# Latent attention: the value products of two steps in one group at every odd step

## The reference

```python
c_q, c_kv = rmsnorm(x @ Wq_down), rmsnorm(x @ Wkv_down)      # 48 and 64 wide
q, k, v   = c_q @ Wq_up, c_kv @ Wk_up, c_kv @ Wv_up          # 16 heads of 128
q_rope, k_rope = rope(x @ Wq_rope), rope(x @ Wk_rope)        # 16 heads of 64
attn = softmax((q @ k.T + q_rope @ k_rope.T) * scale)
out  = (attn @ v) @ Wout
```

## Time and profile before

| | us |
|---|---|
| median of three runs | 2213.99 (2212.3 to 2214.46) |
| the profiled execution | 2221.23 |
| its span | 2219.5 |
| PE busy | 1996.0 (90%) |
| DVE busy | 1276.7 (58%) |
| ACT busy | 817.4 (37%) |
| POOL busy | 867.5 (39%) |
| latent attention, about | 1141 to 2150 of the span |

### The profile page before, as it was taken

One profiled execution on the slowest core, in us unless ns is written; L12 is line 12 of the kernel. 1 busy time (PEld: TensorE's weight loads), 2 busy tenths in 40 slices (PEclk: granted clock), 3 DMA queues, 4 the chain that ended last, 5 costly groups with the idle time before them and its releaser, 6 DMA issues. The chain is left out here.

```text
span 2219.5 us, 29901 instructions
## 1 busy us (share of the span) xinstructions
PE 1996.0 (90%) x8700; PEld 1249.6 (56%) x8701; DVE 1276.7 (58%) x2970; ACT 817.4 (37%) x1549; POOL 867.5 (39%) x684
## 2 busy tenths in 40 slices
PE   5899958898888789986779999999999999999987
PEld 5566635455554756654545555555566555555556
DVE  6322275777775722216656666666656666667525
ACT  2122244554555212223324444444523444444423
POOL 0344311231112034441115556555424555665631
PEclk9999968999899689996769999999999999999999
DMA  9111232232220811124141122222032222212101
GB/s 385 48 58 63 55 126 29 29 44 43 29 29 1 341 52 63 57 54 179 21 95 45 47 57 57 57 57 57 12 75 54 56 58 57 50 44 50 31 1 51
DMA packets 60570, 150.63 MB, mean 68 GB/s; under 512 B 12976, under 2 KB 18304, under 8 KB 58176
## 3 DMA queue, kind: packets, MB, share of 16 engines
q1 hardware_dynamic: 50208, 120.43, 20.6%
q0 software_dynamic: 9120, 24.92, 3.6%
q10 hardware_dynamic: 1152, 4.19, 0.5%
HBM read 68.95 MB, written 18.61 MB: 39 GB/s over the span
## 5 line engine op out<-in xcount | busy, mean ns | idle before, releaser
L1834 POOL TENSOR_TENSOR mla_PS<-mla_PS,mla_PT 128x1024 f32<-128x1024 f32 x192 | 458.4, 2388 | 200.2 <-ACT mla_PT L2120 198.8
L2263 DVE TENSOR_REDUCE mla_MXP<-PS 128x1 f32<-128x512 f32 x512 | 334.4, 687 | 199.7 <-PE PS L1915 197.5
L2120 ACT ACTIVATE mla_PT<-PS 128x512 f32<-128x512 f32 x512 | 293.5, 599 | 421.0 <-PE PS L1935 375.4
L1944 PE MATMUL PS<-mla_PT,mla_CN 128*64 128x512 f32 x1024 | 274.2, 614 | 0.0
L521 DVE COPY moe_HT<-PS 128x512 f32<-128x512 f32 x92 | 63.7, 692 | 307.0 <-PE PS L644 301.2
L1915 PE MATMUL PS<-mla_KH,mla_QH 113*128 113x512 f32 x512 | 199.2, 456 | 18.0 <-DMA mla_KL<-mla_SL 17.8
L675 POOL DMA_INDIRECT moe_XS<-rows_in,moe_GI x96 | 93.7, 976 | 307.5 <-PE PS L630 171.3
L1935 PE MATMUL PS<-mla_QH,mla_KH 113*128 113x512 f32 x512 | 210.3, 411 | 1.7 <-ACT mla_QH L2104 1.5
L1935 PE MATMUL PS<-mla_QL,mla_KH 113*128 113x512 f32 x512 | 201.8, 394 | 0.0
L1935 PE MATMUL PS<-mla_QH,mla_KL 113*128 113x512 f32 x512 | 201.7, 394 | 0.0
L1140 ACT ACTIVATE att_PT<-PS 128x1024 f32<-128x1024 f32 (+1 forms) x192 | 152.3, 812 | 95.2 <-PE PS L975 93.4
(11 more groups left out here) (297 smaller groups left out, 3192.4 us busy)
## 6 DMA issues: line engine op xcount, KB each, us to landing
W<-in_W_dram SPq DMA_DIRECT2D x16, 2048.0 KB, 28.0
mla_QH<-mla_SH SPq DMA_DIRECT2D x64, 128.0 KB, 2.4
mla_KH<-mla_SH SPq DMA_DIRECT2D x64, 128.0 KB, 2.4
mla_QL<-mla_SL SPq DMA_DIRECT2D x64, 128.0 KB, 2.5
mla_KL<-mla_SL SPq DMA_DIRECT2D x64, 128.0 KB, 2.4
mla_KH<-mla_SH SPq DMA_DIRECT2D x64, 96.0 KB, 2.4
mla_KL<-mla_SL SPq DMA_DIRECT2D x64, 96.0 KB, 2.4
sums_Y<-rows_out SPq DMA_DIRECT2D x9, 512.0 KB, 6.0
```

The lines of the kernel that those rows point to most:

```text
L1834: pool.tensor_tensor(PS[:, :], PT[:, slot(0), :] if k == 1 else PS[:, :], PT[:, slot(k), :], ALU.add).then_inc(s_ps.handle, 1)
L1944: ins = pe.matmul(bank(6)[h * DKVL:(h + 1) * DKVL, :], CN[:, b, k, 0:DKVL], PT[:, slot(k), h * HB:(h + 1) * HB], start=(k == 0), stop=(k = ...
L2120: act.activation(PT[:, slot(k), h * HB:(h + 1) * HB], bank(st_bank(s, h))[:, :], ACT.Exp, scale=MLA_SCALE).then_inc(s_p.handle, 1)
L2263: dve.tensor_reduce(MXP[:, n // NPC, c, h, t:t + 1], bank(piece_bank(n))[:, :], AX_X, ALU.max).then_inc(s_mx.handle, 1)
```

## The change

It has these parts, all in the functions `pair` and what they call; each instruction of a pair is still there, on the same engine and with the same operands.

- On PE, `values_of` for steps s-1 and s stands at the end of every odd step s, one after the other; even steps have none. The value unit of step 15, which stood in step 0 of the next pair, is now in step 15.
- The denominators of the block before move from step 0 to step 1 (ahead of the two value units). Those of step 8 stay there and now stand without a value unit behind them.
- `scores_of` takes the head as an argument. From step 10 on, two late pieces stand between the scores of head 0 and head 1 and two behind those of head 1; before, two stood ahead of the value unit and two behind it. At steps 1 to 9 all pieces stand ahead of the value units.
- `EARLY` is {3: 1, 4: 2, 5: 3} instead of {2: 1, 3: 1, 4: 2, 5: 2}; the banks of the early pieces change turns, and piece 26 waits for fewer maxima.
- `project(it + 1, 0, 1)` moves from step 0 to step 1, `project(it + 1, 1, 1)` stands ahead of its step's pieces, `max_rows` moves from step 6 to 7 and from 14 to 15.
- On DVE, the four reciprocals of step 0 spread over steps 1 and 2, between rotation and low parts; `latent_out` is behind them; the products of step 5 move to 4, `rotated` of step 6 to 5, the low parts of step 7 to 6 and 7.
- On ACT the high parts move: two before the exponential of step 2, one after that of step 3, two after that of step 6, one after step 7; `out_copy` stands ahead of the exponentials of steps 0 and 8.

```diff
-    LATE, EARLY = {9: 2, 10: 4, 11: 4, 12: 4, 13: 4, 14: 4, 15: 4}, {2: 1, 3: 1, 4: 2, 5: 2}
+    LATE, EARLY = {9: 2, 10: 4, 11: 4, 12: 4, 13: 4, 14: 4, 15: 4}, {3: 1, 4: 2, 5: 3}
-    piece_bank = lambda n: (A, E)[n % 2] if n >= NLATE else (C, E, B)[n % 3]
+    piece_bank = lambda n: (E, A)[n % 2] if n >= NLATE else (C, E, B)[n % 3]
...
@@ PE, pair
                             near = (it, buf) if s < TB else (it + 1, 1 - buf)
-                            scores_of(it, buf, s, first)
+                            for h in range(2):
+                                scores_of(it, buf, s, h, first)
+                                if s > TB + 1:
+                                    rough_scores(*near, todo[2 * h:2 * h + 2])
...
-                            if s == 0 and not last:
-                                pe.wait_ge(s_mx.handle, s_mx.at(2 * NPC * it + NLATE - 2))
-                                project(it + 1, 0, 0)
+                            if s < 2 and not last:
+                                pe.wait_ge(s_mx.handle, s_mx.at(2 * NPC * it + NLATE - 2 + s))
+                                project(it + 1, 0, s)
                             if s == 8:
                                 denominators(2 * it)
-                            rough_scores(*near, todo[:before])
-                            if s == 0 and not first:
-                                denominators(2 * it - 1)
                             if not last:
                                 if s == 3:
                                     project(it + 1, 0, 2)
+                                if s == 4:
+                                    project(it + 1, 1, 1)
+                            if s <= TB + 1:
+                                rough_scores(*near, todo[:1])
+                            if not last:
                                 if s == 5:
                                     project(it + 1, 1, 0)
                                 if s == 7:
                                     project(it + 1, 1, 2)
-                                if s == 14:
+                            if s <= TB + 1:
+                                rough_scores(*near, todo[1:])
+                            if s % 2:
+                                if s == 1 and not first:
+                                    denominators(2 * it - 1)
+                                if s == 7:
+                                    max_rows(it, 1)
+                                if s == NS - 1 and not last:
                                     pe.wait_ge(s_la.handle, s_la.at(2 * it + 1))
                                     max_rows(it + 1, 0)
-                            if s or not first:
-                                values_of(NS * it + s - 1, 2 * it + (s - 1) // TB, (s - 1) % TB)
...
+                                for done in (s - 1, s):
+                                    values_of(NS * it + done, 2 * it + done // TB, done % TB)
@@ DVE, pair
-                            if s == 5 and not last:
+                            if s == 4 and not last:
                                 products(it + 1, 1, 1)
                             if s == 6:
                                 block_max(it, 1)
-                            if s == 6 and not last:
-                                rotated(it + 1, 1)
+                                if not last:
+                                    lows(it + 1, 1, (0, 1))
+                            if s == 7 and not last:
+                                lows(it + 1, 1, (2,))
                             maxima(near, todo[:1])
                             if s == 5 and not last:
                                 products(it + 1, 1, 0)
+                                rotated(it + 1, 1)
```

More of the change, by code:

```diff
@@ L1923, in max_rows, with scores_of @@
                         ins.then_inc(s_mt.handle, 1)
-                    def scores_of(it, buf, s, first):
+                    def scores_of(it, buf, s, h, first):
                         q, k = s // TB, s % TB
-                        if k == 0:
+                        u = 2 * s + h
+                        if k == 0 and h == 0:
                             pe.wait_ge(s_nm.handle, s_nm.at(2 * (2 * it + q + 1)))
+                        if not (first and u < 3):
+                            pe.wait_ge(s_p.handle, s_p.at(NU * it + freed_unit(u)))
                         qs, ks = slice(q * HB, (q + 1) * HB), slice(k * P, (k + 1) * P)
-                        for h in range(2):
-                            u = 2 * s + h
-                            if not (first and u < 3):
-                                pe.wait_ge(s_p.handle, s_p.at(NU * it + freed_unit(u)))
-                            for n, (kk, qq) in enumerate(((KH, QH), (KH, QL), (KL, QH))):
-                                ins = pe.matmul(bank(st_bank(s, h))[:, :], kk[USED, buf, h, ks], qq[USED, buf, h, qs], start=(n == 0), stop=(n == 2))
-                            ins.then_inc(s_st.handle, 1)
+                        for n, (kk, qq) in enumerate(((KH, QH), (KH, QL), (KL, QH))):
+                            ins = pe.matmul(bank(st_bank(s, h))[:, :], kk[USED, buf, h, ks], qq[USED, buf, h, qs], start=(n == 0), stop=(n == 2))
+                        ins.then_inc(s_st.handle, 1)
                     def values_of(step, blk, k):
@@ L1972, in pair @@
                             todo = pieces_of(s, last)
-                            before = 0 if s == TB + 1 else len(todo) // 2
                             near = (it, buf) if s < TB else (it + 1, 1 - buf)
@@ L2128, in pair @@
                         for s in range(NS):
+                            if s == 0 and not first:
+                                out_copy(2 * it - 1)
+                            if s == 8:
+                                out_copy(2 * it)
                             if not last:
                                 if s == 2:
-                                    highs(it + 1, 0, (1,))
-                                if s == 7:
-                                    highs(it + 1, 1, (1,))
-                                if s == 8:
-                                    highs(it + 1, 1, (2,))
+                                    highs(it + 1, 0, (0, 1))
                                 if s == 12:
@@ L2138, in pair @@
                             exp_of(it, s, first and s < 3)
-                            if s == 0 and not first:
-                                out_copy(2 * it - 1)
                             if not last:
-                                if s == 1:
-                                    highs(it + 1, 0, (0,))
-                                if s == 2:
+                                if s == 3:
                                     highs(it + 1, 0, (2,))
                                 if s == 6:
-                                    highs(it + 1, 1, (0,))
-                                if s == 14:
+                                    highs(it + 1, 1, (0, 1))
+                                if s == 7:
+                                    highs(it + 1, 1, (2,))
+                                if s == NS - 1:
                                     max_copies(it + 1, 1 - buf, 0)
@@ L2296, in pair @@
                                     normalized(after, j)
-                            if s == 0:
-                                if not last:
-                                    products(it + 1, 0, 0)
-                                if not first:
-                                    reciprocals(2 * it - 1, (2, 3, 0, 1))
+                            if s == 0 and not last:
+                                products(it + 1, 0, 0)
+                            if s == 1:
                                 if not last:
                                     products(it + 1, 0, 1)
-                            if s == 1 and not first:
-                                latent_out(2 * it - 1, r - 1, 1)
-                            if s == 5 and not last:
+                                    rotated(it + 1, 0)
+                                if not first:
+                                    reciprocals(2 * it - 1, (2,))
+                                if not last:
+                                    lows(it + 1, 0, (0, 1))
+                                if not first:
+                                    reciprocals(2 * it - 1, (3, 0))
+                            if s == 2:
+                                if not last:
+                                    lows(it + 1, 0, (2,))
+                                if not first:
+                                    reciprocals(2 * it - 1, (1,))
+                                    latent_out(2 * it - 1, r - 1, 1)
+                            if s == 4 and not last:
                                 products(it + 1, 1, 1)
```

34 lines of the change are left out of this document (6 added, 28 removed).

## The result

| | before | after |
|---|---|---|
| median (8 runs each) | 2213.05 us | 2234.85 us |
| lowest to highest | 2212.19 to 2215.53 | 2222.32 to 2240.41 |
| the profiled execution | 2221.23 | 2237.49 |
| its span | 2219.5 | 2235.8 |

The ratio is 1.0090, with a 95% interval of 1.0073 to 1.0106: 20 to 22 us slower. The forecast was +6.3 us, 2220.5, with a range of 2204 to 2236. Direction and place were right; the size is more than three times what I gave. The range held by a narrow margin, and with some luck: the median is 1.2 us under its upper end, three of the eight executions are over it, and the narrower range of my own case, 2215 to 2229, misses the median. The runs of the changed kernel also lie 18 us apart, those of the kernel before 3.3.

A forecast was written before the change was run, and what follows sets the result against it. PE sets the pace, with a once-a-pair loop through the placing DMAs about as long. Twelve middle pairs +5.5, first pairs +3.4, last pairs -1.1 and -1.5 gave +6.3 us: 2220.5, range 2204 to 2236.

The forecast's parts named there:

- my own case: Whole kernel: PE's saving is outweighed by waits, chiefly for placing DMAs; +6.3 us, range 2215 to 2229, chance 0.48.
- The gain: PE's value units and denominators: 16 groups become 9, saving 0.34 each, 2.4 us a pair, if nothing else moved.
- Step 1: Middle pair, first scores of step 0 to step 6: 24.31 becomes 23.74 us.
- the wait of piece 29: At step 4 PE waits 0.3 us (bounds 0 and 0.6) for the maximum of piece 27, delayed by DVE's products.
- Steps 2 and 3: Step 6 to high parts, 3.26, then to piece 0, 9.59 us; PE, there after 11.0, waits 1.8 for placing DMAs.
- Step 4: Piece 0 to step 10: 0.57 becomes 2.42 us, since two value units now stand behind the pieces.
- Step 5: Step 10 to the next step 0: 21.48 becomes 20.56 us; late pieces wait for no maxima.
- First pairs: Two first pairs, with no unit left over from before: five single units become three double ones, +1.7 us each.
- Last pairs: Pairs without placing for their own batch: -1.1 us in batch 1, -1.5 in batch 0, each bounded by 0 and -2.5.
- High parts, reciprocals and out_copy: High parts at steps 2 and 3, reciprocals and out_copy, moved on ACT and DVE, were to cost nothing.
- rival C: PE's clock falls behind the wait at piece 0: 2246 if all 14 pairs lose 1.8 us, 2224 to 2230 if few; chance 0.12.

The follow-up runs named there:

- e10: e5 with the value units taken apart again, one a step, except at steps 7 and 15, which keep two: 2243.16 us, ratio 1.0130 to the kernel before.
- e5: e1 with DVE's products of step 4 put behind the maxima of pieces 27 and 28: 2186.88 us, ratio 0.9885 to the kernel before.
- e1: Changed kernel, but at step 9 the value units of steps 8 and 9 stand ahead of pieces 0 and 1: 2193.56 us, ratio 0.9931.
- e9: Changed kernel, but ACT makes two high parts of half 1 ahead of the exponentials of step 6: 2187.39 us, ratio 0.9878.
- e4: Kernel before, but at step 9 pieces 0 and 1 stand ahead of the value unit of step 8, nothing joined: 2231.64 us, ratio 1.0099.
- e6: e1 with the four late pieces of steps 10 to 15 all behind both heads' scores: 2244.18 us, ratio 1.0145 to the kernel before.
- e7: e1 with the four reciprocals of step 1 in one piece ahead of the rotation: 2246.52 us, ratio 1.0155 to the kernel before.
- e2: Changed kernel with six further score products at step 9 in the 14 pairs that prepare a next one: 2224.49 us, ratio 1.0062.
- e8: Changed kernel with six further score products a pair at step 12, where PE doesn't wait: 2250.48 us, ratio 1.0186.
- e11: e1, e5 and e9 together, with the latent keys of step 3 behind the piece: 2174.99 us, ratio 0.9822 to the kernel before.
- e3: Changed kernel, but ACT instead of SP issues the latent keys' four DMAs of each half: 2201.48 us, ratio 0.9956.

## Why the prediction was right, and what was mis-sized

- The gain (joined units, 0.34 a group): right. e10 shows 0.35.
- Step 1: 23.74 forecast, 23.78 found; the wait of piece 29 was 0.3 (0.3) and cost 0.4, as e5 shows, which took it away. The latent keys of step 7 waited 0.62 (0.6).
- Steps 2 and 3: high parts 27.05 behind step 0, landing 12.8 behind step 6 (12.85). PE's wait was 1.4 to 1.8 in the pairs whose DMAs don't land late; in pairs 1 and 2 it was more, as the late landing was there before and had been partly covered.
- Step 4: 2.53 (2.42) in the pairs at full clock. The first product behind a wait has its successor 0.34 behind it, where I had put 0.23, and 14 times 0.11 is 1.5 of the 2.0 us that lie between 8.3 and 6.3. e1, e9 and e4 show from three sides that the wait at piece 0 is the cause of the loss.
- Step 5: 20.54 (20.56), no late piece waits. e6 shows how close that was: two pieces moved by three products and each double step waits twice.
- First pairs: without the low clock, +1.1 in batch 0 and +2.0 in batch 1 (+1.7 each).
- Last pairs: -1.4 and -1.3 (-1.5 and -1.1).
- High parts, reciprocals and out_copy at nothing: right for the order as it is; e7 shows that the reciprocals' order was needed.
- **What failed is the size of rival C.** I held the low clock for a rival of 0.12, "Mine is 1.8 less the drain, some 1.7, between them", between a wait of 1.44 without a fall and one of 2.23 with it. It belonged into the sum: 10 of 14 pairs had it in the profiled execution, 1.1 to 2.2 us each (16.0 together), against "1.8 us lost" from one row. Added to my case, +6.3 and 16.0 give 22, and 21.8 is the median's difference. So the range held because it reached past my own case, far enough to take in two thirds of rival C. The sum is not quite a proof of the size: e2, whose trace has one slow unit, came out 14 us shorter in the trace and 6 to 8 over the runs. What makes up that difference stays open.

The two rows that I had taken as a scale weren't one. The unit behind a wait of 1.50 ran slowly, that behind 1.56 not (both in the changed kernel); behind 1.26 in e10 it did, behind 2.89 in e8 it didn't. The Trainium skill (TensorE: Matmul & The Clock Gate, Part 1) says that idling brings the throttle back. The rows agree (no slow unit stood in a pair of e11, where PE never idles); which idle time is enough no run here settles.

## What to carry to other kernels

Before work is moved away from a wait, write down what covers that wait now: here one value unit of 1.2 us stood in front of a DMA chain that already ended last, and moving it behind cost 35 to 40 us, where the rest of the change gains 15 to 18 (e1). A wait like these (1.2 to 1.9 us on a full PE) should be priced at its length plus, in many of its cases, 1.6 us for the clock. How many cases one trace doesn't tell: the same waits gave ten slow units in the changed kernel and three in e8. The cheapest cure is to let the chain start earlier (e9: two instructions moved on ACT, 47 us), and then to put independent work ahead of the wait.

## What the runs showed of the hardware

- The granted clock fell to 0.50 at single waits of 1.2 to 3.0 us in an otherwise full PE, though not at all of them: 10 of 14 in the changed kernel, 3 of 14 in e8 with waits as long, 1 of 14 when the wait was filled with six products (e2), 11 of 12 at waits of 1.94 in e7. Most falls cost about 1.6 us, four in e7 3.1. In the changed kernel one set in 0.8 us ahead of piece 0, while PE still waited (from 1299.10 to 1299.80 PE has no product and the granted clock is 0.50), the other nine 0.1 to 1.3 us behind its start.
- More matrix work need not make this program slower: with 84 products more in the waits (e2) the stage is 14 us shorter in the trace and the kernel 6 to 8 us over the runs, barely clear of the noise.
- A second queue that issues small DMAs beside SP's slowed SP's: one issue of 0.86 instead of 0.60, and in most pairs 2.6 to 2.9 from the end of the last issue to piece 0 instead of 1.8 to 2.0 (e3). ACT's own issues stayed at 0.6.
- A group of value units costs PE 0.35 us over and above its products (e10, steps 10 to 15).
